# Block sums of the first stage made by GpSimd between record scatters instead of by a chain on the vector engine

## The reference, cut to what matters

```python
x = x + gnn_attention(layernorm(x), src, dst, Wq, Wk, Wv, ...)   # softmax over the edges that end in a node
x = x + moe(layernorm(x), ...)
x = x + gnn_messages(layernorm(x), edge_attr_4, edge_attr_8, src, dst, ...)
x = x + expert_banks(layernorm(x), ...)
```

## Time and profile before

| what | value |
| --- | --- |
| three runs | 1939.13, 1943.98 and 1942.54 us; median 1942.54 us |
| span of the profiled execution (first to last instruction) | 1941.4 us |
| granted TensorE clock, mean over the span | 0.910 |
| PE, DVE, ACT, POOL busy | 83%, 49%, 36%, 29% of the span |
| first stage (to the first instruction behind its barrier) | 0 to 322.5 us |
| POOL's 157 scatters (L273) | 19.3 to 229.7 us |
| PE's jobs (L417, L420) | 127.2 to 321.6 us |

### The profile page before, as it was taken

The page is one execution under the profiler, slowest core; times in us unless marked ns, Lnnn a source line. Parts: engine busy times, 40 slices in busy tenths (PEclk is TensorE's granted clock), DMA queues, the critical chain, the costliest instruction groups (busy, mean ns, idle before and its releaser), DMA issues. The chain is left out here.

```text
span 1941.4 us, 31644 instructions
## 1 busy us (share of the span) xinstructions
PE 1611.2 (83%) x9860; PEld 1169.5 (60%) x9860; DVE 958.2 (49%) x1950; ACT 701.1 (36%) x1610; POOL 561.3 (29%) x638
## 2 busy tenths in 40 slices
PE   1132298889999999889999999946999999898994
PEld 0111153568888865555999999934555455654662
DVE  8200023967776657654000000065999999632233
ACT  0000032745555543345222221144555555441331
POOL 6777500020110012125000000044555555123133
PEclk6565598989999999889999999968999999998997
DMA  9600011010103030065766554075555555518985
GB/s 292 240 7 6 18 40 41 1 26 18 23 11 82 10 84 2 1 238 163 284 232 234 197 207 171 9 186 142 159 158 152 146 157 155 190 59 270 354 260 185
DMA packets 131143, 252.87 MB, mean 130 GB/s; under 512 B 35344, under 2 KB 52596, under 8 KB 126572
## 3 DMA queue, kind: packets, MB, share of 16 engines
q1 hardware_dynamic: 91692, 171.81, 26.4%
q0 software_dynamic: 39360, 79.86, 14.7%
HBM read 196.03 MB, written 55.52 MB: 130 GB/s over the span
## 5 line engine op out<-in xcount | busy, mean ns | idle before, releaser
L2065 PE MATMUL acc<-prod,ohy 128*64 128x256 f32 x1056 | 250.7, 387 | 13.7 <-issue 7.5
L2109 ACT ACTIVATE ohy<-oh,RECS 128x64 f32<-128x64 f32 x704 | 186.7, 336 | 160.3 <-PE acc L2065 128.2
L2065 PEld LDWEIGHTS acc<-prod,ohy 128*64 128x64 f32 x1056 | 138.9, 138 | 140.0 <-issue 71.5
L2042 POOL DMA_INDIRECT rows<-up_dram,idx x176 | 167.4, 951 | 151.9 <-DVE prod L2183 107.0
L417 PE MATMUL ps<-FT,Wqkv 128*128 128x512 f32 (+1 forms) x192 | 88.1, 591 | 114.3 <-issue 114.3
L2068 PE MATMUL acc<-prod,ohy 128*64 128x256 f32 x704 | 179.6, 397 | 0.0
L273 POOL DMA_INDIRECT rec_dram<-recs,pos x157 | 161.6, 1029 | 60.2 <-issue 48.9
L1819 DVE TENSOR_SCALAR FT<-y_ps,b2T 128x188 f32<-128x188 f32 x32 | 13.2, 414 | 323.3 <-PE y_ps L1768 323.3
L1756 PE MATMUL hid_ps<-FT,W 128*128 128x188 f32 x1024 | 167.7, 325 | 0.7 <-ACT FT L1793 0.7
L2183 DVE TENSOR_TENSOR prod<-w_ps,rows 128x768 f32<-128x768 f32 x176 | 166.8, 948 | 0.0
L1756 PEld LDWEIGHTS hid_ps<-FT,W 128*128 128x128 f32 x1024 | 165.2, 192 | 0.9 <-issue 0.9
(11 more groups left out here) (389 smaller groups left out, 2725.9 us busy)
## 6 DMA issues: line engine op xcount, KB each, us to landing
W<-in_L_ffn_w SPq DMA_DIRECT2D x16, 4096.0 KB, 16.2
bankW_sp<-in_L_ffn_W_sp SPq DMA_DIRECT2D x2, 4096.0 KB, 24.0
xin<-zeros SPq DMA_DIRECT2D x31, 256.0 KB
h_dram<-h3e SPq DMA_DIRECT2D x22, 256.0 KB
h<-h_dram SPq DMA_DIRECT2D x22, 256.0 KB
QF<-q_dram SPq DMA_DIRECT2D x20, 250.0 KB, 4.2
xin_sp<-zeros SPq DMA_DIRECT2D x17, 256.0 KB
xin_fq<-zeros SPq DMA_DIRECT2D x17, 256.0 KB
```

The source lines that it names most:

```text
L2042: pool.indirect_dma_start(out=rows[:, t, :], out_offset=None, in_=up_dram, in_offset=bass.IndirectOffsetOnAxis(ap=idx[:, par, t:t + 1], ax ...
L2065: upper = lambda m: nc.tensor.matmul(acc[0:HALFB, bank, :].rearrange("p (b c) -> p b c", c=MUL)[:, m:4:3 - m, :], ohs[:, 1 + m, :], pr[:, ...
L2109: last = nc.scalar.activation(ohy[:, t % OHY, i, :], oh[:, par, t, :], ACT.Copy, scale=RECS[:, bass.ds(BATCH * g + t, 1), 4 + i])
```

## The change

The two sums are no longer made on DVE. POOL makes them, one instruction behind each odd column of the scatters, for columns 1 to 75. For every b there are two steps, a comparison (`is_ge`, into `passed`, or straight into `odd` or `even` for b = 1 and 2) and an addition to the sum (for b = 1 and 2 only a semaphore increment). That is 19 comparisons and 17 additions of 128x176 elements on POOL, and each waits for the step before it. DVE loses its 19 instructions and waits at their place, before `blockI`, for all 38 steps.

```diff
--- before.py
+++ after.py
@@ -150,7 +150,7 @@
                 done, moved, upper_moved, v_moved = sems_in(st)(
                     "product_done", "product_moved", "upper_moved", "values_moved")
                 q_stored = sems_in(st)("queries_stored0", "queries_stored1")
-                (zeroed,) = sems_in(st)("rows_zeroed")
+                zeroed, sums_steps = sems_in(st)("rows_zeroed", "block_sums")
 
                 srcI, dstI = sb("srcI", [LANES, ECOLS], I32), sb("dstI", [LANES, ECOLS], I32)
                 a4, a8 = sb("a4", [LANES, ECOLS, 4]), sb("a8", [LANES, ECOLS, 8])
@@ -177,7 +177,9 @@
 
                 gI, start = sb("gI", [LANES, BLOCKS], I32), sb("start", [LANES, BLOCKS])
                 numbers = sb("numbers", [LANES, GROUPS])
-                odd, even = sb("odd", [LANES, GROUPS]), sb("even", [LANES, GROUPS])
+                odd, even, passed = sb("odd", [LANES, GROUPS]), sb("even", [LANES, GROUPS]), sb("passed", [LANES, GROUPS])
+                boundaries = [*range(1, BLOCKS, 2), *range(2, BLOCKS, 2)]
+                SUM_STEPS = 2 * len(boundaries)
                 fill = sb("fill", [LANES, ETILES // FILLS, REC])
                 stats, mv = sb("stats", [P, TILES, 6]), sb("mv", [P, TILES, 2])
                 root, rstd = sb("root", [P, TILES]), sb("rstd", [P, TILES])
@@ -231,6 +233,17 @@
 
                     @block.gpsimd
                     def _(pool):
+                        def sum_step(n):
+                            b = boundaries[n // 2]
+                            sums = odd if b % 2 else even
+                            if n % 2 == 0:
+                                out = sums if b in (1, 2) else passed
+                                nc.gpsimd.tensor_scalar(out[:], numbers[:], start[:, b:b + 1], None, ALU.is_ge).then_inc(sums_steps, 1)
+                            elif b in (1, 2):
+                                pool.sem_inc(sums_steps, 1)
+                            else:
+                                nc.gpsimd.tensor_tensor(sums[:], sums[:], passed[:], ALU.add).then_inc(sums_steps, 1)
+
                         nc.gpsimd.memset(srcI[:, EMAIN:], 0)
                         nc.gpsimd.memset(dstI[:, EMAIN:], -1)
                         nc.gpsimd.memset(a4[:, EMAIN, :], 0.0)
@@ -273,6 +286,11 @@
                             pool.indirect_dma_start(
                                 out=rec_dram, out_offset=bass.IndirectOffsetOnAxis(ap=pos[0:rows_of, c:c + 1], axis=0),
                                 in_=recs[0:rows_of, c, :], in_offset=None).then_inc(scattered[batch % 2], 16)
+                            if c % 2 == 1 and c // 2 < SUM_STEPS:
+                                n = c // 2
+                                if n >= 1:
+                                    pool.wait_ge(sums_steps, n)
+                                sum_step(n)
                         for b in range(2):
                             mine = sum(1 for c in range(ECOLS) if c // BATCH % 2 == b)
                             pool.wait_ge(scattered[b], 16 * mine)
@@ -353,13 +371,8 @@
                                                     ALU.subtract, ALU.mult).then_inc(applied, 1)
 
 
-                        every = numbers[:]
-                        for sums, first in ((odd, 1), (even, 2)):
-                            step(nc.vector.tensor_scalar(sums[:], every, start[:, first:first + 1], None, ALU.is_ge))
-                            for b in range(first + 2, BLOCKS, 2):
-                                step(nc.vector.scalar_tensor_tensor(out=sums[:], in0=every, scalar=start[:, b:b + 1], in1=sums[:],
-                                                                    op0=ALU.is_ge, op1=ALU.add))
                         nc.vector.memset(blockI[:, 0:1], 0)
+                        dve.wait_ge(sums_steps, SUM_STEPS)
                         step(nc.vector.tensor_tensor(blockI[:, 1:], odd[:], even[:], ALU.add))
                         step(nc.vector.tensor_scalar(turnI[:, 1:], blockI[:, 1:], 1.0, None, ALU.add))
                         step(nc.vector.tensor_scalar(spotI[:], blockI[:, 1:], REGIONS - 1, None, ALU.bitwise_and))
```

## The result

The changed kernel takes 1884.48 us, the median of four runs (1880.57 to 1889.86). The kernel before took 1943.26 in the runs beside them (four, 1939.13 to 1947.27). The ratio is 0.970, with a 95% interval of 0.968 to 0.972: 58.8 us faster, where 51 less and 1892 were predicted. The profiled execution is the longest of the four, with a span of 1888.2 us against 1941.4 before.

The account below looks back on a forecast made before the run. PE's 34 jobs were taken to end the first stage, slowed by reports queued behind POOL's scatters. Prompt reports, less PE's pause and later slow time, end it at 271 against 321.6: 1942.5 - 51, rounded 1892 us, range 1868 to 1912.

Parts of the forecast that it names:

- The lag of the reports: First stage: ACT hears of PE's work tens of microseconds late, one PE instruction being reported in each 1.40 us.
- DVE's chain, 0: DVE loses 19 instructions at 53 to 72 us; hidden under PE's jobs, so worth 0.
- POOL's operations: POOL gains 19 comparisons at 0.39 us and 17 additions at 0.57, 17.1 us in sum; alone they cost 0.
- The cost of a first call: Some 6 us at the first call of freshly loaded GpSimd code, as the Trainium skill states; left out.
- The gaps: Up to column 75 a scatter pair takes 3.0 us, so PE is reported promptly and starts jobs about 62, not 127.
- the need: Time each POOL scatter takes in what it shares with completion reports: about 1.40 us, 2.8 a pair.
- The point of decision: Added POOL time per scatter pair from which reports come through promptly: 0.26 us.
- the thin margin: A pair at 3.0 us on POOL against 2.8 required: only 0.2 us idle per pair.
- the slower rival: POOL's new operations queue with the scatters or are too short; slow time ends 17.1 us later: 1957 us, chance 0.19.
- the queue: Scatters waiting because POOL issues them 0.13 us faster than they pass; a waiting PE instruction passes only once per scatter.
- The added wait: DVE waits at `blockI` for POOL's sums until 142.3, delaying key subtractions; PE stands from 119 to 150.
- The queue's return: After column 75 PE slows again from 156 to 255, one job per 22.4 us; the stage ends at 271.

Follow-up runs that it names:

- the kernel with 256 columns: Kernel before plus an idle 256-column POOL memset behind each odd scatter column up to 75, DVE's chain kept: 1912.19 us, ratio 0.9865.
- at 1.315: Kernel before plus an idle 128-column POOL memset behind each odd scatter column up to 75, 1.315 us a scatter: 1937.89 us, ratio 0.9983.
- at 1.41: Kernel before plus an idle 656-column POOL memset behind every fourth scatter column up to 75, 1.41 us a scatter: 1895.1 us, ratio 0.9742.
- At 1.425: Kernel before, sums and tables on DVE behind the keys, 384-column memsets behind odd columns to 75 or to 91: 1868.19 and 1874.73 us.
- the kernel with 1 column: Kernel before plus an idle 1-column POOL memset behind each odd scatter column up to 75: 1940.28 us, ratio 0.9998.

## Why the prediction was right, step by step

The lag of the reports, its cause in the spacing of the scatters, and the cure by time on POOL were right; the experiments show each apart. The size was 7.8 us short of the measured gain (51 against 58.8). Step by step:

1. *DVE's chain, 0.* Right: moved alone it gives a ratio of 1.0003.

2. *POOL's operations.* An addition took 0.56, as worked out from its price per element. The comparison was mis-sized: 0.74 us and not 0.39. I had put the one-input operation below the two-input one, as they stand at 2 elements with 0.22 and 0.20, and that row already had it the other way round. The 36 operations come to 19 x 0.74 + 17 x 0.56 = 23.6 us, not 17.1. It cost only 3.6 us in the end of the sums (145.9 against 142.3) and 2.8 in the last scatter (249.6 against 246.8). An operation lengthened its pair by a little less than it took (0.70 and 0.53 us, 22.3 in all), the scatters began 0.9 us earlier (18.3 against 19.3), and fewer of them were slow of themselves. A memset gives back more: 0.33 us of it lengthened a pair by 0.18, as 0.14 of the 0.30 between two scatters goes where it stands. That second price I had not looked for, and it put the kernel with 256 columns at 1.365 and not at 1.435, which I take for the reason that its expectation failed; the wider gap alone was not run. The cost of a first call, which I left out, did not show: the first comparison took 0.74 us and the first addition 0.56, with no idle time before them.

3. *The gaps.* A pair took 3.07 to 3.24 us, above the need. The point of decision was put at 0.26 us per pair (1.40 a scatter). It is not a point: at 1.315 the reports are half relieved until 92 us and not behind that, at 1.365 they hold for 10 to 20 us, at 1.41 for some 35, and at 1.58 all the way. At 1.425 they hold for some 40; then a triple of key jobs takes 10.0 to 12.1 us until 135 in one kernel (ACT's copies 3.5 to 4.3 us apart) and 16 to 17 in the other (5.0 to 5.7 us a job from 96 to 134), where the prompt pace is 8.4. The change stood at 1.58, 0.18 above 1.40, where I had 0.10 (3.0 a pair), so the thin margin that spoke for the slower rival was thicker. That was luck in part: the comparison that I priced too low is what made it so. No kernel ran at the predicted 1.50, and between 1.425, where the reports slip, and 1.58 nothing shows whether it would have held. That rival's other leg, that POOL's operations join the queue and lengthen the slow time, falls with the kernel with 1 column, as far as a memset may stand for them: with 38 of them the slow time ends at 245.26, against 243.44. But POOL's own increments can come late like PE's (1.7 us there).

The need itself comes out at or a little under 1.40. With half the rows POOL's last scatters are 1.40 apart, while PE has reports to make. In the changed kernel the queue is empty at the end of the sums, if the gaps work, and 81 scatters later, at 255.66, PE is free: (255.66 - 145.85)/81 = 1.36. The kernel with the tables behind the keys gives (255.21 - 146.36)/81 = 1.34, with nothing from PE to report from 158 on; that holds the barrier too, so it is an upper bound. Half of the scatters gives 1.27 + 3.8/60 = 1.33 at the least, with some 60 scatters since 50 us and 3.8 us of slow time behind the last one (123.68 to 127.45), and 1.43 if it lasted until the first queries (133.58). The two kernels with gaps of 0.43 us give 1.38 and 1.39 from their last gap to PE's release, if their queue was empty at that gap, which their reports say it was not quite.

The jobs began at 56.2 and not 62. One cover came out better than I said: SP's issue of zeros, which I left at 96.4, was over at 79.85, so the store of the queries held ACT only to 85.24, and once more to 87.81, and PE ran on without a gap. The timeline of SP:

```profile
66.77 13.08 SPq L1609 DMA_DIRECT2D xin_fq<-zeros  x17
79.89 11.64 SPq L229 DMA_DIRECT2D q_dram<-QT  x8
```

The same 17 DMAs took 23.24 us to issue before, 1.37 each; now it is 0.77 each. It goes by the gaps: 22.4 to 23.1 us with the chain moved, with 1 column and with half the rows, 14.8 with 128 columns, and 12.8 to 13.1 in all with 256 columns and more. SP was held up by the scatters' rhythm too.

4. *The added wait.* PE stood from 113.65 to 149.82, predicted 119 to 150. The sums ended 3.6 us later than predicted, and the eight tables took 2.5 us and not 5.6, for I had priced them at DVE's rate under the scatters' queue, which was empty here.

5. *The queue's return.* It bites at about 160 (job 22 is copied promptly at 159.99; job 23 is copied 7.3 us behind it, where a job of its width takes 1.5), predicted 156; it is over at 255.66, predicted 255. Reports stand 21.7 to 22.4 apart, as said. By then 192 + 37 + 28 matmuls or 32.1 jobs are issued, predicted 30.4. That 1.7 jobs at 3.43 make 5.8 us, and it is the whole difference between the predicted end at 271 and the measured 265.3. I had 26 jobs issued when the slow time begins; 28.6 stood issued at 177.4, since the queue bit 4 us later and PE did three jobs behind its pause before that, not two.

The rule of the Trainium skill ("TensorE: Matmul & The Clock Gate", "The cost: per-tile semaphore tail") that speaks against the change, some 26 ns for an increment, is not borne out as a bound: ACT heard of PE's last transposes 41.65 us late before, and promptly after.

What is not settled: what it is that scatters and reports share. The runs show that its cost is fixed per scatter and not per row, and that it holds back PE, DVE, SP and POOL's own increments; they do not show where it sits, nor why the reports slip at 1.365 to 1.425 beside a busy PE, and by different amounts in two kernels with the same gaps, while the drains above put the need at 1.34 to 1.36, where PE reports no more than one instruction per scatter. That each report takes a small share itself would fit, and no run measured it.

## What to carry to other kernels

If an engine seems to wait for nothing while a row of indirect DMAs goes out on GpSimd at 1.2 to 1.3 us each, compare the rhythm of the waiting engine with theirs: one instruction per DMA is the sign, and time put between the DMAs (here 0.43 us per pair, beside the tables moved out of PE's way, or work that has to be done anyway) is worth more than it costs, as long as another engine has work to report. Put those gaps where the other engines are busy, and drop them where only the DMAs are left, since the stage can't end before these have drained. When work moves to a cheaper place, look at what stands behind its consumer: the wait for the sums cost PE 36 us here, of which some 7 to 10 were on the path.

## What the runs showed of the hardware that I had not expected

- The delay is per indirect DMA: with 64 rows in each and not 128, POOL issues one each 1.19 us and not 1.27 (until it is held to 1.40 itself), while the slow time ends at the same place (244.65 and 243.44).
- A one-input comparison with a scalar per partition took 0.74 us on POOL for 128x176 elements, a two-input addition 0.56. Memsets of 1, 128, 256, 384 and 656 columns took 0.12, 0.22, 0.33, 0.43 and 0.66 us.
- An increment of POOL itself can be late as well: with memsets of 1 column, two of them waited 1.70 and 1.71 us for the one before.
- Behind a compute operation an indirect DMA of POOL starts after 0.17 us, behind another indirect DMA after 0.30.
- SP's issue of DMAs is slow as well beside scatters at 1.27 us each: 17 fills in 23.24 us, and in 13.08 beside scatters at 1.58.
